# Longer lags between the stages of two rank-and-store passes of a graph kernel, and another order of the stages within a turn

## The chip, the cores and the metric

The kernel runs on one core of one Trainium2 chip. The metric is the device time of one execution, in microseconds. Three executions of the kernel before took 5831.21, 5831.95 and 5836.04 us; the median is 5831.95 us. Below, PE is the tensor engine, DVE the vector engine, ACT the scalar engine, POOL GpSimd, and SP the engine that issues most of the plain DMAs.

## What is computed

Four graph layers follow one another on 3125 nodes with 128 features and 53125 edges (25000 random edges, the same reversed, and a loop for each node, sorted by `dst`). Each layer is followed by a residual sum and a layer norm:

```python
edge_index = jnp.stack([src, dst])
x = _layernorm(x + _L0_gnn_ref(x, edge_index, edge_attr_32, ...), axis=-1)   # attention over dst, 8 heads
x = _layernorm(x + _L1_gnn_ref(x, src, dst, ...), axis=-1)                   # normalised sum over src
x = _layernorm(x + _L2_gnn_ref(x, edge_attr_64, edge_index, ...), axis=-1)   # attention over nodes and edges
x = _layernorm(x + _L3_gnn_ref(x, node_vec, ..., src, dst), axis=-1)         # two softmaxes over dst
```

The sums and maxima over segments need the edges grouped by `src` in some layers and by `dst` in others. The kernel therefore sorts the edges twice, ahead of all layers, and only these two sorting passes are touched by the change.

## The kernel before

**Tiles.** Edges are taken 128 to a tile and four tiles to a group (G = 4). The first pass ("src") has 104 groups, the second ("dst") has 110. A pass takes each group of 512 edge rows, works out the slot of each row among the rows with the same key (its rank), and scatters the rows into a table in HBM with one indirect DMA per tile.

**The stages of one group** are functions in `ranks` (L561 to L641) and are the same in both passes:

- `dve_onehots` (L571): DVE writes the one-hot matrices of the low key part, `so16` (L574), and of the high part, `hi16` (L576).
- `pe_transpose` (L603, matmuls of L609): PE turns `so16` over, into half of PSUM bank 2.
- `copy_out` (L631, L636): ACT copies that into `rohT_keys[k]`, of which there are four.
- `pe_same` (L612, L616): PE multiplies the turned one-hots with themselves, into bank 6 or 7.
- `dve_mask` (L580, L583): DVE masks the result into `ssame`.
- `pe_rank` (L620, L625 and L627): PE makes the slot numbers, into bank 3, of which there is one.
- `dve_pick` (L586, L589 and L595): DVE multiplies with `hi16` and reduces into `stage[k]`, four buffers. The reduction waits until the scatter of four groups earlier has landed.
- `scatter` (L651, L655) on POOL issues the four indirect DMAs of the group out of `pay[k]`, four buffers. `load` (L647) on SP fills `pay[k]` once the scatter of four groups earlier has landed.

In the first pass ACT has one more stage, `ids` (L671, L673). In the second pass `grown_rows` (L681 to L744) adds the key and value rows of the source node to each edge row:

- `onehots` (L692, L694) on DVE, `transposes` (L705, L709) on PE into the other half of bank 2, `copies` (L712, L715) on ACT.
- `kv` (L717, L723): PE first loads four block numbers into registers (L777), then does 12 matmuls of 257 columns into banks 0, 1, 4 and 5, one set for all groups, so it waits until `keep` of the group before is done.
- `keep` (L728, L732): two ACT copies out of those four banks into `pay[k]`, then, after a wait for `products`, one small copy (L737) that releases the scatter.
- `products` (L697, L699 and L702) on DVE.

**What sets the order.** Every engine executes its own list in order. `stepwise` (L537) gives each engine a list of pairs (lag, stage). In turn N the engine runs down its list, and a pair with lag d works on group N - d. Four turns are one body of a hardware loop (`run`, L348); two bodies are written out ahead of it (lead=2). Waits on semaphores tie the engines together. The two lists of the kernel before are

```python
return {"vector": [(4, dve_pick), (2, dve_mask), (0, dve_onehots)],                             # L639
        "tensor": [(1, pe_same), (3, pe_rank), (0, pe_transpose)], "scalar": [(0, copy_out)],
return loads, {"vector": [(3, products), (1, onehots)], "tensor": [(3, kv), (1, transposes)],   # L743
               "scalar": [(3, keep), (1, copies)]}, ready, (s_td, s_tc)
```

In the second pass `together` (L746) puts the list of `ranks` ahead of that of `grown_rows`. A turn is thus: PE `pe_same`, `pe_rank`, `pe_transpose`, `kv`, `transposes`; ACT `copy_out`, `keep`, `copies`; DVE `dve_pick`, `dve_mask`, `dve_onehots`, `products`, `onehots`.

**The shared bank.** PE must not write PSUM bank 2 while ACT reads it, and in the second pass two transposes land there. So `pe_transpose` of group n waits for `copies` of group n - 2 (L607: s_tc of the grown rows at n - 1), and `copy_out` of group n waits for `transposes` of group n - 1 (L634: s_td of the grown rows at n).

Of the kernel before, what the change touches and what calls it, by code (L numbers as in the profile page):

```python
# [25 lines left out]
P = 128  # L26
# [20 lines left out]
G = 4  # L47
# [8 lines left out]
def wait(eng, sem, value):  # L56

    if isinstance(value, int) and value <= 0:
        return
    eng.wait_ge(sem, value)  # L60
# [30 lines left out]
def gnn_program(nc, x, keys, edge_attr, node_vec, Wqkv, WeT, L1_kernel, L1_bias, W_node,  # L91
                W_nodeT, W_edge, W_edgeT, a_node, a_edge, L3_W, L3_b, out):
    ctx = ExitStack()
    with ctx:
# [466 lines left out]
        def ranks(o, bank_shared=None):  # L561
# [9 lines left out]
            def dve_onehots(v, n, k):  # L571
                wait(v, s_td, n - 1)
                wait(v, s_ps, n - 3)
                nc.vector.tensor_tensor(so16[k % 2][:, :, :], iota0[:, None, :].to_broadcast([P, G, P]),  # L574
                                        key[o]["lo"][:, bass.ds(n * G, G)].to_broadcast([P, G, P]), ALU.is_equal)
                nc.vector.tensor_tensor(hi16[k][:, :, :], iota0[:, None, 0:NH].to_broadcast([P, G, NH]),  # L576
                                        key[o]["hi"][:, bass.ds(n * G, G)].to_broadcast([P, G, NH]),
                                        ALU.is_equal).then_inc(s_oh, 1)

            def dve_mask(v, n, k):  # L580
                v.wait_ge(s_sd, n + 1)
                wait(v, s_gd, n - 1)
                nc.vector.tensor_tensor(ssame[k % 2][:, :, :], ps[6 + k % 2][:, :].rearrange("p (g n) -> p g n", g=G),  # L583
                                        after[:, None, :].to_broadcast([P, G, P]), ALU.mult).then_inc(s_su, 1)
# [18 lines left out]
            def pe_transpose(pe, n, k):  # L603
                pe.wait_ge(s_oh, n + 1)
                wait(pe, s_tc, n)
                if bank_shared:
                    wait(pe, bank_shared[1], n - 1)  # L607
                for j in range(G):
                    last = nc.tensor.transpose(turned(k)[:, j * P:(j + 1) * P], so16[k % 2][:, j, :], ident16[:, :])  # L609
                last.then_inc(s_td, 1)  # L610
# [20 lines left out]
            def copy_out(act, n, k):  # L631
                act.wait_ge(s_td, n + 1)
                if bank_shared:
                    wait(act, bank_shared[0], n)  # L634
                wait(act, s_gd, n - 3)
                nc.scalar.copy(rohT_keys[k][:, :, :], turned(k)[:, 0:G * P].rearrange("p (g n) -> p g n", g=G)) \  # L636
                  .then_inc(s_tc, 1)

            return {"vector": [(4, dve_pick), (2, dve_mask), (0, dve_onehots)],  # L639
                    "tensor": [(1, pe_same), (3, pe_rank), (0, pe_transpose)], "scalar": [(0, copy_out)],  # L640
                    "placed": s_ps}  # L641

        def scatter_rows(o, loads, to, width, ready, placed):
# [16 lines left out]

            return {"sync": [(0, load)], "pool": [(4, scatter)]}

        def own_rows():
# [14 lines left out]

            return loads, {"scalar": [(2, ids)]}, ready

        def grown_rows():  # L681

# [22 lines left out]
            def transposes(pe, n, k):  # L705
                pe.wait_ge(s_oh, n + 1)
                wait(pe, s_tc, n)
                for j in range(G):
                    last = nc.tensor.transpose(beside_ranks[:, j * P:(j + 1) * P], oh16[k % 2][:, j, :], ident16[:, :])  # L709
                last.then_inc(s_td, 1)  # L710
# [29 lines left out]
            def ready(g, n, k):  # L740
                hold(g, s_up, n + 1, passed["pool"])

            return loads, {"vector": [(3, products), (1, onehots)], "tensor": [(3, kv), (1, transposes)],  # L743
                           "scalar": [(3, keep), (1, copies)]}, ready, (s_td, s_tc)  # L744

# [610 lines left out]
        for c in range(5):  # L1356
            with nc.Block() as block:
                @block.vector
                def _(v):
# [5 lines left out]
        cleared = key_starts("dst", table2)  # L1365
        loads, parts, ready, turned_beside = grown_rows()
        placing = ranks("dst", turned_beside)
        run((stepwise("dst", together(placing, parts, scatter_rows("dst", loads, table2, ROW2, ready, placing["placed"])),
                      cleared), 0, T // (4 * G), 1), lead=2)
# [371 lines left out]
```

## Time and profile before

| what | before |
|---|---|
| median of three executions | 5831.95 us |
| the profiled execution's own time | 5880.84 us |
| its span from first to last instruction | 5879.0 us |
| PE busy / DVE busy / POOL busy / ACT busy | 51% / 41% / 38% / 15% of the span |
| first pass, first to last scatter | 236.5 to 880.8 us |
| second pass, first to last scatter | 1085.6 to 1811.5 us |
| granted PE clock over the whole span | 0.531 of full |

The profiled execution took 48.89 us more than the median. Every duration in this document that is not a run's time comes from such an execution. An engine can be idle because it waits for nothing that matters; the busy shares say only that no engine is full over the whole span, and the two passes have to be read by themselves.

### The profile page before, as it was taken

How to read it: one execution, taken by the hardware profiler on the slowest of the kernel's cores; microseconds unless marked ns; L12 is line 12 of the kernel's file. 1: busy time of each engine (PE TensorE's matmuls, PEld its weight loads, DVE VectorE, ACT ScalarE, POOL GpSimd, SP SyncE). 2: the span in 40 equal slices, each digit the busy share in tenths (PEclk: the TensorE clock that was granted, in tenths of full speed). 3: DMA queues.
4: the chain of work that ended last, by engine and by line, in shares of the span. 5: the costliest groups of instructions: out<-in, count | busy, mean ns of one | idle time of the engine just before them, and what ended most of it. 6: DMA issues, size and time to landing. Idle time of an engine off the chain costs nothing. (4 is left out here: it accounts for less than half of the span.)

```text
span 5879.0 us, 79222 instructions
## 1 busy us (share of the span) xinstructions
PE 3027.2 (51%) x17772; PEld 2505.0 (43%) x17773; DVE 2436.1 (41%) x5186; ACT 893.0 (15%) x2414; POOL 2253.2 (38%) x2513
## 2 busy tenths in 40 slices
PE   2222222466664555399756665333334999633332
PEld 1111111344443444289745555222223999423332
DVE  7733337655554444644522222422225555422224
ACT  1211111333332222100000000111111222100000
POOL 0266660466662000000047776366660000056763
PEclk6555555566665555555555555555555555555555
DMA  0122223444442222123211112122222334111112
GB/s 20 47 64 65 64 62 8 153 140 141 140 143 74 65 65 65 33 66 77 54 38 43 44 44 39 31 42 43 43 42 39 82 84 86 30 41 45 45 45 36
DMA packets 639690, 365.32 MB, mean 62 GB/s; under 512 B 456808, under 2 KB 589970, under 8 KB 639634
## 3 DMA queue, kind: packets, MB, share of 16 engines
q0 software_dynamic: 83712, 175.08, 10.9%
q1 hardware_dynamic: 381682, 131.90, 10.1%
q10 hardware_dynamic: 174240, 57.69, 4.2%
q8 instruction: 23, 0.38, 0.0%
q14 instruction: 33, 0.27, 0.0%
HBM read 229.22 MB, written 135.24 MB: 62 GB/s over the span
## 5 line engine op out<-in xcount | busy, mean ns | idle before, releaser
L1102 PE MATMUL banks<-both,pool 128*128 128x128 f32 x3520 | 1198.2, 478 | 423.1 <-DVE both L1681 423.1
L1102 PEld LDWEIGHTS banks<-both,pool 128*128 128x128 f32 x3520 | 918.5, 332 | 479.5 <-issue 455.5
L1066 POOL COPY stage<-slots 128x4 int32 (+1 forms) x220 | 43.0, 196 | 1921.4 <-ACTq L383 1920.2
L655 POOL DMA_INDIRECT table<-pay_own,stage x432 | 442.0, 1023 | 748.6 <-DVE stage L595 294.2
L1099 PEld LDWEIGHTS banks<-pool 128*128 128x128 f32 x1760 | 475.7, 330 | 288.9 <-issue 288.9
L1099 PE MATMUL banks<-pool 128*128 128x11 f32 (+1 forms) x1760 | 398.2, 299 | 255.6 <-DVE pool L1468 251.2
L761 POOL DMA_INDIRECT pool<-y_table,stage x440 | 445.2, 1012 | 188.9 <-issue 170.3
L761 POOL DMA_INDIRECT pool<-n_table,stage x440 | 438.3, 996 | 190.7 <-issue 154.3
L655 POOL DMA_INDIRECT table<-q,stage x424 | 431.5, 1018 | 188.6 <-issue 125.4
L761 POOL DMA_INDIRECT pool<-z_table,stage x440 | 430.6, 979 | 188.8 <-issue 116.8
L1078 DVE TENSOR_TENSOR pool<-iota,slots 128x512 f32<-128x512 f32 x440 | 302.7, 688 | 340.0 <-PE banks L1102 294.5
L616 PE MATMUL banks<-acc 128*128 128x128 bf16 x856 | 118.8, 286 | 596.2 <-ACT acc L636 310.0
L589 DVE TENSOR_TENSOR acc<-banks,acc 128x208 f32<-128x208 f32 x214 | 80.1, 374 | 742.6 <-PE banks L627 389.0
L616 PEld LDWEIGHTS banks<-acc 128*128 128x128 bf16 x856 | 67.5, 123 | 650.2 <-issue 442.8
L723 PE MATMUL banks<-pool,both 128*128 x1320 | 292.6, 407 | 30.2 <-issue 17.9
L1681 DVE TENSOR_TENSOR both<-pool,slot_tmp 128x512 f32<-128x512 f32 x110 | 76.2, 692 | 505.9 <-DMA pool<-z_table,stage 505.9
L636 ACT COPY acc<-banks 128x512 bf16<-128x512 bf16 x214 | 125.4, 586 | 1045.4 <-issue 430.4
L1025 ACT COPY acc<-banks 128x512 f32<-128x512 f32 (+1 forms) x12 | 5.0, 487 | 1767.2 <-PEq L383 1767.2
L1467 DVE TENSOR_SCALAR both<-pool 128x512 f32<-128x512 f32 x110 | 55.2, 502 | 524.3 <-DMA pool<-y_table,stage 524.3
L1102 PE MATMUL banks<-acc 128*128 128x64 f32 x880 | 242.1, 438 | 0.0
L1102 PEld LDWEIGHTS banks<-acc 128*128 128x128 f32 x880 | 235.6, 335 | 3.4
L723 PEld LDWEIGHTS banks<-pool,both 128*128 128x128 bf16 x1320 | 177.8, 135 | 119.0 <-issue 54.5
(333 smaller groups left out, 5668.3 us busy)
## 6 DMA issues: line engine op xcount, KB each, us to landing
pay_own<-table SPq DMA_DIRECT2D x110, 332.0 KB, 3.1
pool<-table ACTq DMA_DIRECT2D x110, 256.0 KB, 2.9
h_rows<-pool SPq DMA_DIRECT2D x110, 128.0 KB
acc<-table SPq DMA_DIRECT2D x110, 128.0 KB, 2.3
pool<-h_rows ACTq DMA_DIRECT2D x110, 128.0 KB, 2.9
pay_own<-table ACTq DMA_DIRECT2D x110, 128.0 KB, 2.6
pay_own<-table SPq DMA_DIRECT2D x56, 200.0 KB
q<-table SPq DMA_DIRECT2D x54, 200.0 KB
```

What stands on the lines that cost most here:

```text
L589: nc.vector.tensor_tensor(sprod[:, :, :].rearrange("p g (n s) -> p g n s", s=2), rank_bank(k).rearrange("p (g n s) -> p g n s", g=G, s=2), ...
L616: last = nc.tensor.matmul(ps[6 + k % 2][:, j * P:(j + 1) * P], rohT_keys[k][:, j, :], rohT_keys[k][:, j, :], start=True, stop=True)
L636: nc.scalar.copy(rohT_keys[k][:, :, :], turned(k)[:, 0:G * P].rearrange("p (g n) -> p g n", g=G)) \
L655: nc.gpsimd.indirect_dma_start(to, bass.IndirectOffsetOnAxis(ap=stage[k][:, j:j + 1], axis=0), pay[k][:, j, 0:width], None).then_inc(lande ...
L723: last = nc.tensor.matmul(kv_of[j], rohT[k % 2][:, j, :], kv16[:, bass.ds(blocks[j], 1), part, :].rearrange("p o d -> p (o d)"), start=par ...
L761: nc.gpsimd.indirect_dma_start(to, None, table_ap, bass.IndirectOffsetOnAxis(ap=index, axis=0)) \
L1066: nc.gpsimd.tensor_copy(stage[h][:, :], index[:, bass.ds(i * (2 * G) + h * G, G)]).then_inc(s_st, 1)
L1078: nc.vector.tensor_tensor(buf["oh"][h][:, :, :], iota1[:, None, :].to_broadcast([P, G, P]), lo1[o][:, t].to_broadcast([P, G, P]), ALU.is_e ...
L1099: nc.tensor.matmul(banks[:, bass.ds(blocks[j] * SIDE + (7 * 512 + side0), side_cols)], buf["oh"][h][:, j, :], buf["side"][h][:, j, 0:side_ ...
L1102: last = nc.tensor.matmul(banks[:, bass.ds(blocks[j] * P + col0, cols)], buf["oh"][h][:, j, :], buf["rhs"][h][:, j, 0:cols], start=False, ...
L1467: nc.vector.tensor_scalar(rhs[h][:, :, :], grow[h][:, :, 0:D], 1.0, None, ALU.mult)
L1681: return nc.vector.tensor_tensor(rhs[h][:, :, :], grow[h][:, :, 0:D], bc(slot_tmp[0][:, t], [P, G, D]), ALU.mult)
```

## The change

Seven things are edited. (1) In `ranks` the lags become 6, 4, 0 on DVE, 3, 5, 1 on PE and 2 on ACT. (2) The one-hot `hi16` moves from `dve_onehots` to `dve_mask`, with its wait for `stage` of four groups earlier. (3) `pe_transpose` waits for the grown `copies` one group further back, and `copy_out` for the grown `transposes` one group further back. (4) The grown `transposes` get a new wait, for `copy_out` of group n + 1 (s_tc of the ranks at n + 2). (5) The grown lags become 5 and 2 on DVE, 5 and 3 on PE, 6 and 4 on ACT. (6) The lags of `ids` and `scatter` become 5 and 7. (7) In the second pass a hand-written `order` replaces the plain joining of lists: PE now runs `pe_same`, `pe_rank`, `kv`, `pe_transpose`, `transposes`; ACT `keep`, `copy_out`, `copies`; DVE `dve_pick`, `dve_mask`, `products`, `onehots`, `dve_onehots`.

```diff
             def dve_onehots(v, n, k):
                 wait(v, s_td, n - 1)
+                nc.vector.tensor_tensor(so16[k % 2][:, :, :], iota0[:, None, :].to_broadcast([P, G, P]),
+                                        key[o]["lo"][:, bass.ds(n * G, G)].to_broadcast([P, G, P]),
+                                        ALU.is_equal).then_inc(s_oh, 1)
+
+            def dve_mask(v, n, k):
                 wait(v, s_ps, n - 3)
-                nc.vector.tensor_tensor(so16[k % 2][:, :, :], iota0[:, None, :].to_broadcast([P, G, P]),
-                                        key[o]["lo"][:, bass.ds(n * G, G)].to_broadcast([P, G, P]), ALU.is_equal)
+                wait(v, s_gd, n - 1)
                 nc.vector.tensor_tensor(hi16[k][:, :, :], iota0[:, None, 0:NH].to_broadcast([P, G, NH]),
-                                        key[o]["hi"][:, bass.ds(n * G, G)].to_broadcast([P, G, NH]),
-                                        ALU.is_equal).then_inc(s_oh, 1)
-
-            def dve_mask(v, n, k):
+                                        key[o]["hi"][:, bass.ds(n * G, G)].to_broadcast([P, G, NH]), ALU.is_equal)
                 v.wait_ge(s_sd, n + 1)
-                wait(v, s_gd, n - 1)
                 nc.vector.tensor_tensor(ssame[k % 2][:, :, :], ps[6 + k % 2][:, :].rearrange("p (g n) -> p g n", g=G),
...
                 if bank_shared:
-                    wait(pe, bank_shared[1], n - 1)
+                    wait(pe, bank_shared[1], n - 2)
...
                 if bank_shared:
-                    wait(act, bank_shared[0], n)
+                    wait(act, bank_shared[0], n - 1)
...
-            return {"vector": [(4, dve_pick), (2, dve_mask), (0, dve_onehots)],
-                    "tensor": [(1, pe_same), (3, pe_rank), (0, pe_transpose)], "scalar": [(0, copy_out)],
+            return {"vector": [(6, dve_pick), (4, dve_mask), (0, dve_onehots)],
+                    "tensor": [(3, pe_same), (5, pe_rank), (1, pe_transpose)], "scalar": [(2, copy_out)],
+                    "copied": s_tc,
...
-            return {"sync": [(0, load)], "pool": [(4, scatter)]}
+            return {"sync": [(0, load)], "pool": [(7, scatter)]}
...
-            return loads, {"scalar": [(2, ids)]}, ready
+            return loads, {"scalar": [(5, ids)]}, ready
...
                 pe.wait_ge(s_oh, n + 1)
                 wait(pe, s_tc, n)
+                pe.wait_ge(ranks_copied[0], min(n + 2, groups_of["dst"]) if isinstance(n, int) else n + 2)
...
-            return loads, {"vector": [(3, products), (1, onehots)], "tensor": [(3, kv), (1, transposes)],
-                           "scalar": [(3, keep), (1, copies)]}, ready, (s_td, s_tc)
+            return loads, {"vector": [(5, products), (2, onehots)], "tensor": [(5, kv), (3, transposes)],
+                           "scalar": [(6, keep), (4, copies)]}, ready, (s_td, s_tc)
...
-        run((stepwise("dst", together(placing, parts, scatter_rows("dst", loads, table2, ROW2, ready, placing["placed"])),
+        ranks_copied.append(placing["copied"])
+        order = {"vector": [placing["vector"][0], placing["vector"][1], parts["vector"][0], parts["vector"][1], placing["vector"][2]],
+                 "tensor": [placing["tensor"][0], placing["tensor"][1], parts["tensor"][0], placing["tensor"][2], parts["tensor"][1]],
+                 "scalar": [parts["scalar"][0], placing["scalar"][0], parts["scalar"][1]]}
+        run((stepwise("dst", together(order, scatter_rows("dst", loads, table2, ROW2, ready, placing["placed"])),
```

No buffer is added: every tile and every instruction of a group stays, and only their order and their waits differ.

## Rows read from the trace of the kernel before

**Rows 1.** Busy time by stretch; columns: stretch, length, PE, PEld, DVE, ACT, POOL, clock, DMA, GB/s

```profile
237.00:882.00 645.00, 149.10 (x1616) 116.98 (x1616) 211.79 (x505) 70.80 (x202) 412.68 (x416) 0.50 0.23 64
1085.00:1813.00 728.00, 481.51 (x3448) 339.49 (x3448) 371.57 (x857) 231.98 (x541) 460.36 (x440) 0.64 0.44 141
```

**Rows 2.** Instructions of L655, both passes: duration in ns min/median/max, first and last start

```profile
L655 POOL DMA_INDIRECT table<-pay_own,stage x208: 956/962/1479, 236.5 to 870.7; - x104
L655 POOL DMA_INDIRECT table<-q,stage x208: 955/962/1422, 247.5 to 880.8; - x104
...
L655 POOL DMA_INDIRECT table<-pay_own,stage x224: 955/963/1336, 1085.6 to 1811.5; - x112
```

**Rows 3.** Groups by line, 442 to 842 us: busy, mean ns | idle before, releasers

```profile
L655 POOL DMA_INDIRECT table<-pay_own,stage x129 | 129.3, 1002 | 105.9 <-DVE stage L595 75.7 <-issue 30.2
```

**Rows 4.** POOL's timeline, first pass: start, us, engine, line; idle time before

```profile
657.12 0.96 POOL L655 DMA_INDIRECT table<-q,stage  x1 [0.30 <-issue]
663.02 1.10 POOL L655 DMA_INDIRECT table<-pay_own,stage  x1 [4.94 <-DVE stage L595]
```

**Rows 5.** DVE's timeline, first pass, the two picks before that gap

```profile
650.80 0.38 DVE L589 TENSOR_TENSOR acc<-banks,acc 128x208 f32<-128x208 f32 x1 [7.29 <-remote]
...
661.04 0.38 DVE L589 TENSOR_TENSOR acc<-banks,acc 128x208 f32<-128x208 f32 x1 [8.07 <-PE banks L627]
```

**Rows 6.** PE's timeline, same stretch

```profile
643.63 0.58 PE L609 MATMUL banks<-ident,acc 128*128 128x128 bf16 x4
659.25 0.61 PE L616 MATMUL banks<-acc 128*128 128x128 bf16 x4 [15.04 <-issue]
```

**Rows 7.** ACT's timeline, same stretch

```profile
658.61 0.59 ACT L636 COPY acc<-banks 128x512 bf16<-128x512 bf16 x1 [15.79 <-remote]
```

**Rows 8.** Groups by line, 1200 to 1700 us

```profile
L655 POOL DMA_INDIRECT table<-q,stage x152 | 159.7, 1051 | 81.2 <-issue 41.6 <-ACT ge_src L737 39.5
```

**Rows 9.** PE's timeline, second pass, one turn and the start of the next

```profile
1642.78 0.61 PE L616 MATMUL banks<-acc 128*128 128x128 bf16 x4 [3.26 <-ACT acc L636]
...
1643.51 0.22 PE L627 MATMUL banks<-acc 128*128 128x26 bf16 x1
1644.27 0.61 PE L609 MATMUL banks<-ident,acc 128*128 128x128 bf16 x4 [0.53 <-ACT both L715]
1644.97 2.76 PE L723 MATMUL banks<-pool,both 128*128 x12
1647.52 0.52 PE L709 MATMUL banks<-ident,both 128*128 128x128 bf16 x4
1648.84 0.40 PE L616 MATMUL banks<-acc 128*128 128x128 bf16 x4 [0.81 <-issue]
...
1651.25 1.04 PE L723 MATMUL banks<-pool,both 128*128 x4 [0.37 <-issue]
```

**Rows 10.** ACT's timeline, second pass, same stretch

```profile
1642.06 0.59 ACT L636 COPY acc<-banks 128x512 bf16<-128x512 bf16 x1 [6.13 <-issue]
...
1648.20 0.59 ACT L636 COPY acc<-banks 128x512 bf16<-128x512 bf16 x1 [3.99 <-PE banks L709]
1648.69 1.09 ACT L732 COPY pay_own<-banks 128x514 f32<-128x514 f32 x2
```

**Rows 11.** POOL's timeline, second pass

```profile
1651.94 1.25 POOL L655 DMA_INDIRECT table<-pay_own,stage  x1 [0.30 <-issue]
...
1656.99 0.96 POOL L655 DMA_INDIRECT table<-q,stage  x1 [0.97 <-issue]
```

**Rows 12.** DVE's timeline, second pass, beside those scatters

```profile
1651.68 0.68 DVE L574 TENSOR_TENSOR acc<-iota,raw 128x512 bf16<-128x512 f32 x1
...
1652.45 0.42 DVE L699 TENSOR_TENSOR acc<-q,wge 128x256 f32<-128x256 f32 x1
...
1653.24 0.68 DVE L694 TENSOR_TENSOR both<-iota,slots 128x512 bf16<-128x512 f32 x1
```

**Rows 13.** Instructions of L574, second pass: first and last start

```profile
L574 DVE TENSOR_TENSOR acc<-iota,raw x110: 679/682/733, 1071.8 to 1777.0; 128x512 bf16<-128x512 f32 x110
```

More of the change, by code:

```diff
@@ L572, in dve_onehots @@
                 wait(v, s_td, n - 1)
-                wait(v, s_ps, n - 3)
                 nc.vector.tensor_tensor(so16[k % 2][:, :, :], iota0[:, None, :].to_broadcast([P, G, P]),
-                                        key[o]["lo"][:, bass.ds(n * G, G)].to_broadcast([P, G, P]), ALU.is_equal)
-                nc.vector.tensor_tensor(hi16[k][:, :, :], iota0[:, None, 0:NH].to_broadcast([P, G, NH]),
-                                        key[o]["hi"][:, bass.ds(n * G, G)].to_broadcast([P, G, NH]),
+                                        key[o]["lo"][:, bass.ds(n * G, G)].to_broadcast([P, G, P]),
                                         ALU.is_equal).then_inc(s_oh, 1)
             def dve_mask(v, n, k):
+                wait(v, s_ps, n - 3)
+                wait(v, s_gd, n - 1)
+                nc.vector.tensor_tensor(hi16[k][:, :, :], iota0[:, None, 0:NH].to_broadcast([P, G, NH]),
+                                        key[o]["hi"][:, bass.ds(n * G, G)].to_broadcast([P, G, NH]), ALU.is_equal)
                 v.wait_ge(s_sd, n + 1)
-                wait(v, s_gd, n - 1)
                 nc.vector.tensor_tensor(ssame[k % 2][:, :, :], ps[6 + k % 2][:, :].rearrange("p (g n) -> p g n", g=G),
@@ L677, in ready, with grown_rows @@
                 hold(g, s_id, n + 1, passed["pool"])
-            return loads, {"scalar": [(2, ids)]}, ready
-        def grown_rows():
+            return loads, {"scalar": [(5, ids)]}, ready
+        def grown_rows(ranks_copied):
             s_pl = [sem(f"sorted_rows_loaded{k}") for k in range(4)]
@@ L1365, in gnn_program @@
         cleared = key_starts("dst", table2)
-        loads, parts, ready, turned_beside = grown_rows()
+        ranks_copied = []
+        loads, parts, ready, turned_beside = grown_rows(ranks_copied)
         placing = ranks("dst", turned_beside)
-        run((stepwise("dst", together(placing, parts, scatter_rows("dst", loads, table2, ROW2, ready, placing["placed"])),
+        ranks_copied.append(placing["copied"])
[3 more added lines that the diff above has]
+        run((stepwise("dst", together(order, scatter_rows("dst", loads, table2, ROW2, ready, placing["placed"])),
                       cleared), 0, T // (4 * G), 1), lead=2)
```

## The prediction

> **What bounds it now.** The busy shares name no bound, so the two touched passes are read by stretch: POOL is busy for 413 of 645 us in the first and 460 of 728 in the second, and PE, at half its clock in the first and 0.64 in the second, for 149 and 482 [rows 1]. POOL's work is the scatters. First to last start is 644.3 us in the first pass, over 103.75 groups (the last start is the fourth of a group) 6.21 us a group, and 725.9 us in the second, over 109.75 groups 6.61 [rows 2]. Against this stand POOL's own times. A scatter takes 1.002 us on average in the steady part of the first pass [rows 3] and 1.051 in the second [rows 8], with 0.30 between two of them [rows 4, 11]. Four make 5.21 and 5.40 us a group: the floor that POOL sets. What lies above it, 1.00 and 1.21 us a group, is waiting: 104 and 133 us. Nothing else in the kernel is touched.
>
> **First pass: who is late?** In one loop body of four groups (25 us) POOL runs back to back and then idles 4.94 us for the slot numbers in `stage` [rows 4]. Its supplier, DVE's pick, waited 7.29 us and then 8.07 us for `pe_rank` [rows 5]. PE's rows show the transposes of a group issued at 643.63, but ACT, which waits only for them, starts at 658.61, after 15.79 us idle; PE's next row is at 659.25 [rows 6, 7]. So PE's results came 14.4 us after the modelled end of its work, though no engine owed it anything. What holds PE there no row says. I call it the gap; a pass of 26 bodies has about one each.
>
> **Second pass: who is late?** Here PE and ACT take turns. The row of `kv` is 2.76 us; then PE waits 0.81 for ACT's `copy_out`, and its `pe_transpose` waits 0.53 for ACT's `copies` [rows 9]. ACT in turn starts `copy_out` only when PE's `transposes`, behind `kv`, are done (releaser L709, 3.99 idle), and `keep` (1.09 us) stands behind it [rows 10]. The bank that the two transposes share makes each engine finish its turn before the other starts: 6.06 us from 1642.78 to 1648.84. POOL idles 0.97 before the next group [rows 11].
>
> **The change, part by part.** The sum is made against the profiled execution (5880.84 us); it lies 48.89 above the median of 5831.95, and I carry the difference over unchanged.
>
> (a) *Second pass, lags, order and the two relaxed waits.* With the transposes of one turn released by the copies of the same turn, but `kv` put ahead of them, ACT's `keep`, `copy_out` and `copies` run beside PE's `pe_same`, `pe_rank` and `kv`. `kv` needs only `keep` of the group before, which starts when the previous `kv` ends and takes 1.09; PE has two sets of transposes and two small stages, 2.08 us by [rows 9] (0.95, 0.61, 0.52), in between. The new wait of `transposes` for `copy_out` is met too: ACT is through with its turn two copies of 0.59 [rows 7, 10] after PE's last turn, while PE is in `kv`. Behind it on PE stand `pe_same` and `pe_rank`, which DVE's pick needs a turn later, so a turn of slack covers them. PE then waits for nobody and is bound by its work: from 1642.78 to 1643.73, and from 1644.27 to 1648.04, 4.72 us [rows 9]. To this comes the load of the block numbers, until now under the transposes but for 0.37 us [rows 9]; behind `pe_rank` it is bare, between 0.37 and 0.75 us (that row and its cover of 0.38), and I take 0.5: 5.2. The gap exists here also, smaller: `copy_out` found 6.13 instead of 3.99 us idle, 2.14 more [rows 10], about once in four groups, 0.5 a group. Together 5.7, a little above POOL's 5.40. I take 5.7: (6.61 - 5.7) x 110 = -100 us. Ends: 5.40, POOL's floor, if the gap hides in the four buffers or PE's clock is granted more often: -133. And 6.3, where only the 0.53 and no more of the waits goes: -34.
>
> (b) *First pass, lags.* Work and buffers stay; one bank still holds the ranks, so PE can't run ahead of the pick. `pe_rank` no longer stands behind a `pe_same` whose copy has just been made. After the gap ACT's copy (0.59) and the start of `pe_same` came first: copy at 658.61, `pe_same` at 659.25 [rows 6, 7]. That start, 0.64 us, goes once in a body: 26 x 0.65 = -17 us. Ends: 0, and -104 if the gap itself came from the order and POOL reaches its floor.
>
> (c) *`hi16` moved to the mask stage.* The same instruction on DVE, which is busy 51% of the second pass [rows 1]; its wait for `stage` is met two turns earlier. Nothing, and 0.26 us of DVE a group has that idle half as cover.
>
> (d) *`scatter` and `ids` lags 7 and 5.* Per-engine bookkeeping; POOL's list has one stage, and SP's loads keep lag 0, their place and their wait, so each queue issues as before. Nothing in the steady state.
>
> (e) *Filling.* The first scatter came 13.8 us after the first one-hots, with lag 4 [rows 2, 13]: 3.45 a turn. Two more turns are at most 7 us a pass, 14 in all; the first turns do less work, so I take 10. At the end POOL drains last either way. Ends: 0 and 14.
>
> Sum: -100 - 17 + 10 = -107; 5880.84 becomes 5774, the median 5725.
>
> **A rule against it.** Scatters beside DVE work are longer, 1.25 us against 0.96, but the neighbours of that row run through three DVE instructions at no more than this [rows 11, 12]. By the rows the cost is fixed per group and is in the 5.40. The Trainium skill (SBUF — State Buffer, Who interferes with whom) says that a DVE instruction with two SBUF inputs and a GpSimd instruction that reads SBUF take an exclusive port, the loser blocked for the whole instruction. That rule would matter more the closer the two engines are packed; by it the sum would be that of rival 5.
>
> **Rivals.**
> 1. *The gap belongs to the old order.* PE sat at a wait for ACT while it lasted [rows 6]; if it needs that, both passes reach POOL's floor: -104 - 100 or -133, + 10, 5605 to 5638. For it: the busier PE of the second pass has a short gap, not a long one. Against it: the waits in other turns of the first pass cost nothing.
> 2. *PE and ACT still alternate.* If sharing the bank binds through the new wait, a turn is 6.3: -34 - 17 + 10, 5791. Against it: the waits name stages a turn back.
> 3. *Slower: the long gap moves into the second pass.* There PE is to be the bound, and nothing hides a gap. The place is `kv` behind `pe_rank`. Four turns are 4 x 5.2 + g; the old four are 26.4, so it decides from g = 5.6 us. With the 8.07 of [rows 5] four turns are 28.9, 7.22 a group: +67 - 17 + 10, 5892. Against it: today's second pass has 2.14.
> 4. *The change does nothing*, as another wait binds PE and ACT at the old pace: 5832, within 6.
> 5. *Slower, the port.* DVE's three instructions of [rows 12], 0.68 + 0.42 + 0.68, each blocking POOL in full on top of 4 x (0.96 + 0.30) = 5.04, make 6.82 a group: +23, with (b) and (e) 5848. Today's scatters bear out a fifth of it.
>
> **How the numbers follow.** Forecast 0.55; rivals 1 to 5: 0.20, 0.15, 0.05, 0.03, 0.02. A measurement of this kernel tells 0.2%, some 12 us, from no change. Faster: 0.90; same: 0.03; slower: 0.07. The forecast's own ends of (a) and (b) give about 5690 to 5765. The range takes in rival 2, and rival 1 down to 5620, where its better half starts; outside stay that half and the slow cases, under 0.2: 5620 to 5805.
>
> **What would show it.** In the second pass: PE's `pe_transpose` no longer released by L715, `kv` rows directly behind L627, a turn of 5.2 to 5.7 us, ACT starting `keep` ahead of `copy_out`, scatters 5.4 to 5.8 us a group. In the first pass: the 15 us without a PE row still there, POOL's idle time about 4.3 instead of 4.94, 6.0 to 6.1 a group. I am wrong if the first pass loses its gap, if PE's turns stay above 6 us, or if the time between the passes moves.

## The result and the profile after

Over five executions of each, the kernel before took 5836.04 us (median; 5831.21 to 5842.58) and the changed one 5862.96 us (5859.70 to 5868.44): ratio 1.0046, 95% interval 1.0031 to 1.0061. The change made the kernel **0.46% slower**, where 1.8% faster was predicted and 5620 to 5805 us was the range.

The profiled execution of after took 5864.28 us (span 5862.5). That of before took 5880.84, some 45 more than its median, so the two profiles side by side show a gain of 16.6 us where the medians show a loss of 27. The stretches have to be compared with this in mind.

The two passes of after by stretch and its scatters, first pass, then second; they answer to [rows 1, 2]:

```profile
237.00:925.00 688.00, 181.67 (x1740) 128.26 (x1740) 240.32 (x578) 79.89 (x234) 410.97 (x416) 0.50 0.29 61
1085.00:1800.00 715.00, 386.58 (x3334) 301.46 (x3331) 365.27 (x832) 224.05 (x521) 429.68 (x424) 0.74 0.44 139
```

```profile
L656 POOL DMA_INDIRECT table<-pay_own,stage x208: 955/962/1429, 236.2 to 852.8; - x104
L656 POOL DMA_INDIRECT table<-q,stage x208: 955/962/1470, 247.3 to 862.9; - x104
```

```profile
L656 POOL DMA_INDIRECT table<-pay_own,stage x224: 957/963/1452, 1066.1 to 1806.6; - x112
...
  ACT ge_src L739: 371.1, 53
  issue: 123.1, 385
```

The first pass takes 862.9 - 236.2 = 626.7 us (before 644.3), the second 1806.6 - 1066.1 = 740.5 (before 725.9). In the second, POOL waits 53 times for ACT's small copy (L739), once in two groups; the 371.1 us contain some 203 between the passes (1066.1 - 862.9), so a wait is (371.1 - 203.2) / 52 = 3.2 us. Counted in the two traces, POOL stops for more than 2 us between two scatters 18 times in the second pass of before and 52 times in that of after. POOL's timeline shows the pattern, eight scatters back to back and then a stop (answers to [rows 11]):

```profile
1432.88 0.96 POOL L656 DMA_INDIRECT table<-q,stage  x1 [3.23 <-ACT ge_src L739]
...
1440.95 0.96 POOL L656 DMA_INDIRECT table<-q,stage  x1 [0.31 <-issue]
1442.21 0.96 POOL L656 DMA_INDIRECT table<-q,stage  x1 [0.30 <-issue]
```

The PE, ACT and DVE timelines of the same turns (answer to [rows 9, 10, 12]):

```profile
1436.43 2.03 PE L725 MATMUL banks<-pool,both 128*128 x12
1438.30 0.38 PE L609 MATMUL banks<-ident,acc 128*128 128x128 bf16 x4
1438.52 0.39 PE L711 MATMUL banks<-ident,both 128*128 128x128 bf16 x4
...
1440.44 0.20 PE L627 MATMUL banks<-acc 128*128 128x26 bf16 x1
1445.78 0.61 PE L725 MATMUL banks<-pool,both 128*128 x2 [5.14 <-ACT pay_own L734]
```

```profile
1435.01 1.08 ACT L734 COPY q<-banks 128x514 f32<-128x514 f32 x2 [1.97 <-PE banks L725]
...
1444.45 1.08 ACT L734 COPY pay_own<-banks 128x514 f32<-128x514 f32 x2 [7.29 <-remote]
```

```profile
1444.61 0.69 DVE L695 TENSOR_TENSOR both<-iota,slots 128x512 bf16<-128x512 f32 x1 [2.68 <-remote]
```

The turn is the one that was planned: `kv` (L725), both transposes, and `keep` first on ACT. But `kv` ends at 1438.46 by the model and `keep`, which waits for it and for the load of its rows, starts at 1444.45; that load was issued at 1426.44, 18 us before, and in no group of this pass less than 15 us before; the transposes issued at 1438.52 (L711) release DVE only at 1444.61. PE had issued all of it by 1440.44. By the signals in the trace the results of `kv`, both transposes, `pe_same` and `pe_rank` came at 1444.38, 1444.43, 1444.49, 1444.55 and 1444.65, 1.2 to 1.5 us after POOL's last scatter ended (1442.21 + 0.96 = 1443.17). The rows of those transposes are 0.22 us apart, the signals 0.06: the work had been done, and its results were held. It is not this turn alone: of the 110 `keep` stages of this pass, 55 start more than 2 us after both `kv`'s modelled end and ACT's own last instruction, and 48 of these 55 start 1.2 to 1.5 us after the end of POOL's last scatter; only two start while POOL goes on issuing. This is the gap of the prediction, 6 us long, once in **two** groups: the cycle from 1432.88 to the next start after a stop, 1446.44, is 13.56 us, 6.78 a group. The Trainium skill (Perfetto Trace Analysis, Tensor Engine Instruction) says that a matmul's end in a profile is estimated, and that its semaphore is pushed only when PSUM has acknowledged the write. The trace agrees in so far as the modelled end came 6 us ahead of the first reader.

### The profile page after: what moved, and what is told of

Same layout as the page of the kernel before. It is cut to its first block and busy times, and to the rows that moved or that the text cites. A ratio compares the mean times of both kernels' runs of the same rounds, so it can differ in the third digit from the quotient of the medians.

```text
span 5862.5 us, 79114 instructions
## 1 busy us (share of the span) xinstructions
PE 2965.0 (51%) x17772; PEld 2482.8 (42%) x17773; DVE 2436.9 (42%) x5186; ACT 896.3 (15%) x2414; POOL 2239.7 (38%) x2513
## 5 line engine op out<-in xcount | busy, mean ns | idle before, releaser
L725 PE MATMUL banks<-pool,both 128*128 x1320 | 252.6, 362 | 239.1 <-ACT pay_own L734 127.8
L625 PE MATMUL banks<-work,acc 128*128 (+1 forms) x856 | 123.3, 219 | 367.3 <-issue 183.5
L725 PEld LDWEIGHTS banks<-pool,both 128*128 128x128 bf16 x1320 | 160.9, 122 | 301.9 <-issue 247.7
L625 PEld LDWEIGHTS banks<-work,acc 128*128 128x128 bf16 x856 | 86.3, 108 | 406.3 <-issue 399.2
L609 PE MATMUL banks<-ident,acc 128*128 128x128 bf16 x856 | 117.0, 283 | 239.7 <-ACT acc L636 120.5
```

Of the source, the lines that this page charges most:

```text
L625: nc.tensor.matmul(to, rohT_keys[k][:, j, :], pairs[o][:, :, bass.ds(n * G + j, 1), :] .rearrange("p h t s -> p h (t s)"), start=True, sto ...
L725: last = nc.tensor.matmul(kv_of[j], rohT[k % 2][:, j, :], kv16[:, bass.ds(blocks[j], 1), part, :].rearrange("p o d -> p (o d)"), start=par ...
```

## The experiments

The kernel before itself has two times, on one and the same chip and unchanged: about 5670 us when PE's results come in time, and 5830 to 5872 when they come late during the scatters. Kernels that were timed together on one chip, within some minutes, make one occasion here. Each run below stands beside the kernel before of its own occasion; "first" and "second" are the times from first to last scatter start of the passes, out of its profile. "Late" and "in time" are told from the traces: where the kernel before takes 5670 us, no copy of the transposes in the first pass (L636) starts more than 0.2 us after both the modelled end of the transposes and ACT's own last instruction; where it takes 5830 or more, 36 to 52 of the 104 start more than 2 us after them, in every run but e13.

| occasion | kernel | median us | ratio (95%) | first | second |
|---|---|---|---|---|---|
| record, late | before | 5836.0 | | 644.3 | 725.9 |
| | full change | 5863.0 | 1.0046 (1.0031–1.0061) | 626.7 | 740.5 |
| 1, in time | before (e1: 5671.4, one execution) | 5669.7 | | 539.2 | 666.0 |
| | e2 first pass only | 5672.3 | 1.0001 (0.9991–1.0012) | 542.3 | 665.2 |
| | e3 second pass only | 5584.4 | 0.9849 (0.9836–0.9863) | 540.0 | 579.5 |
| | e4 narrow rows | cut off | | 543.5 | 588.4 |
| 2, in time | e5 full change | 5583.2 | 0.9847 (0.9833–0.9861) | 543.3 | 581.7 |
| | e6 lags only | 5661.1 | 0.9985 (0.9976–0.9994) | 542.9 | 651.7 |
| 3, late (before 5871.7) | e7 full, more PE work | 6049.9 | 1.0302 (1.0282–1.0322) | 637.5 | 913.9 |
| | e8 before, more PE work | 5982.1 | 1.0187 (1.0168–1.0207) | 643.1 | 835.2 |
| | e9 order only | 5929.4 | 1.0096 (1.0077–1.0116) | 642.3 | 788.0 |
| 4, late (before 5833.3) | e10 full change | 5859.8 | 1.0047 (1.0030–1.0064) | 624.7 | 739.5 |
| | e11 lags only | 5834.7 | 1.0001 (0.9990–1.0011) | 624.9 | 717.4 |
| | e12 narrow rows | cut off | | 625.4 | 737.6 |
| | e13 all landed | 6024.6 (one run) | | 712.0 | 818.4 |
| 5, in time (before 5668.7) | e14 three landed | 5703.8 | 1.0062 (1.0045–1.0079) | 582.7 | 658.3 |
| | e15 small instruction | 5719.1 | 1.0088 (1.0071–1.0104) | 610.7 | 646.3 |
| 6, in time (before 5668.0) | e16 three landed | 5702.1 | 1.0061 (1.0044–1.0078) | 582.1 | 657.4 |
| | e17 order only | 5618.1 | 0.9909 (0.9892–0.9925) | 539.4 | 614.6 |
| 7, late (before 5830.8) | e18 three landed | 5793.9 | 0.9930 (0.9914–0.9947) | 620.7 | 687.6 |

Occasions 2, 3, 6 and 7 were on the same chip, within an hour: in time, late, in time, late, the last two less than three minutes apart.

### One pass at a time (e1 to e4)

e1 is the kernel before. e2 and e3 choose the old or the new lags, waits, order and place of `hi16` by pass:

```diff
+NEW = {"src": True, "dst": False}      # e2; e3 the other way round
...
-                    wait(pe, bank_shared[1], n - 2)
+                    wait(pe, bank_shared[1], n - (2 if NEW[o] else 1))
```

> The kernel before, unchanged, for a second profile. The first profiled execution took 5880.84 us against a median of 5836. Theory A (the second pass slowed by more than the first gained, and the first profile of before was a slow example): this execution takes about 5836 us, its passes are some 10 to 45 us shorter than in the first profile (first pass under 644, or second under 726 us from first to last scatter). Theory B (the passes are as in the first profile, and the change loses time elsewhere): the passes again take 644 and 726 us, whatever the total.

> Only the first pass has the new lags; the second is as before. Theory A: the first pass gains a little (first to last scatter about 627 us as in the profile of the changed kernel), so the time is 10 to 20 us below before. Rival B (the deeper lags cost in both passes): 5 to 20 us above before.

> Only the second pass has the new lags, order and waits; the first is as before. Theory A: the second pass holds the loss, 35 to 50 us above before (27 measured for both plus what the first pass gained). Rival B: about half of the 27 us, 10 to 15 above before.

None of the three expected pictures came, because the gap was gone and with it 166 us of the kernel before. The first pass takes 539.2 / 103.75 = 5.20 us a group there, POOL's floor as predicted (5.21), with nothing left to gain. The second gains 86.5 us and lands at 579.5 / 109.75 = 5.28, its floor. So the change does what it was meant to do, and the loss on record is not in its turns as such.

e4 cuts the changed kernel off behind the second pass (all four layers are left out) and lets the second pass write 16 columns of each row to a narrow table:

```diff
-                    nc.gpsimd.indirect_dma_start(to, ...
-                                                 pay[k][:, j, 0:width], None)
+                    nc.gpsimd.indirect_dma_start(thin if o == "dst" else to, ...
+                                                 pay[k][:, j, 0:16 if o == "dst" else width], None)
```

> The changed kernel, ended after the second pass (all four layers left out), whose scatters put only 16 of 358 columns of each row into a narrower table: as many scatter instructions on POOL, a twentieth of their bytes. Theory T (PE's results are held back by the traffic of the scatters): in the second pass the gap of about 6 us between the issue of kv and ACT's keep in every second group goes, and a group takes 5.0 to 5.6 us. Theory P (they are held back by POOL's own scatter instructions, or by the order of the waits): the gap stays, two groups still take about 13.5 us.

Where nothing is late it says nothing about the gap; e12 is the same kernel on a late occasion.

### The whole change, and its lags without its order (e5, e6)

```diff
+        order = together(placing, parts)      # e6
         run((stepwise("dst", together(order,
```

> The whole change, unchanged, in the same comparison as the next kernel. Theory A: the change is worth what its second pass is worth (5584.4 against 5669.7 us, -85), since on the chip of the last runs the first pass already runs at POOL's pace: ratio 0.985, no stretch without PE rows, second pass 5.3 us a group. Theory B: the two longer passes disturb each other or the place where the second starts: ratio above 0.99 though PE's results come in time. Theory C: this is a chip where PE's results come late during the scatters, as in the two traces on record: kernel before near 5836 us, ratio 1.003 to 1.006, and results of PE come late once in two groups in the second pass.

> The whole change but for its hand-written order: in the second pass the lists are joined plainly, so PE runs pe_transpose ahead of kv, ACT copy_out ahead of keep. Theory L, the longer lags alone take PE and ACT out of each other's turns: as the full change, second pass 5.3 us a group (ratio 0.985 where PE's results come in time). Theory O, kv has to stand ahead of the transposes, or PE waits with it for keep of the same turn and ACT for PE: second pass 6.0 us a group or more, ratio 1.00 or a little below.

e5 is theory A: 0.9847. Its scatters and their waits in the second pass; POOL's idle time is nearly all its own 0.30 us between scatters:

```profile
L656 POOL DMA_INDIRECT table<-pay_own,stage x224: 957/963/1488, 983.3 to 1565.0; - x112
...
  ACT ge_src L739: 203.6, 6
  issue: 125.0, 410
```

Nearly all of the 203.6 us in 6 waits is the time between the passes (983.3 - 780.2 = 203.1). PE, ACT and POOL in one turn of e5:

```profile
1419.82 0.63 PE L609 MATMUL banks<-ident,acc 128*128 128x128 bf16 x4
1420.25 0.63 PE L711 MATMUL banks<-ident,both 128*128 128x128 bf16 x4
...
1422.45 1.68 PE L725 MATMUL banks<-pool,both 128*128 x12 [0.49 <-ACT both L717]
```

```profile
1420.12 1.08 ACT L734 COPY pay_own<-banks 128x514 f32<-128x514 f32 x2 [4.24 <-PE banks L725]
...
1424.22 1.08 ACT L734 COPY pay_own<-banks 128x514 f32<-128x514 f32 x2 [1.96 <-PE banks L725]
```

```profile
1419.40 0.96 POOL L656 DMA_INDIRECT table<-q,stage  x1 [0.30 <-issue]
...
1424.47 0.96 POOL L656 DMA_INDIRECT table<-q,stage  x1 [0.31 <-issue]
```

`keep` starts 0.10 us after `kv`'s modelled end (1418.74 + 1.28 = 1420.02), where in after it starts 6 us late. e6 comes out near theory O (6.0 us a group or more): without the order PE and ACT take turns again, 5.94 us a group. PE and ACT of e6:

```profile
1431.62 0.38 PE L609 MATMUL banks<-ident,acc 128*128 128x128 bf16 x4 [1.75 <-ACT both L717]
...
1434.92 0.63 PE L711 MATMUL banks<-ident,both 128*128 128x128 bf16 x4
```

```profile
1435.64 0.58 ACT L636 COPY acc<-banks 128x512 bf16<-128x512 bf16 x1 [4.17 <-issue]
```

This is rival 2 of the prediction, for the lags alone: `pe_transpose` ahead of `kv` waits for the copies, and ACT idles 4.17 us behind `kv` before `copy_out`.

### More work for PE, and the order alone (e7, e8, e9)

```diff
-                for j in range(G):                                          # pe_same
+                for j in list(range(G)) * (13 if o == "dst" and k % 2 else 1):
```

> The whole change, and in the second pass pe_same of every second group repeats its four matmuls 13 times in place of once (same result), some 5 us more of PE at half its clock, which is what the trace of the changed kernel on record shows PE's results late by, once in two groups. Theory G, that lateness alone accounts for its 740.5 us: the pass goes from 580 us to between 700 and 760 (two groups 13 to 13.8 us), the kernel to about 5700 to 5770. Theory S, the buffers and longer lags swallow a stall of this size: the pass stays below 620 us.

> The kernel before with the same repeated matmuls. If PE and ACT alternate there, nothing hides them: the pass grows by all of it, 55 times some 5 us: from 666 to about 900 us or more, ratio 1.04. Then the lateness on record, which costs the old order only 60 us in this pass and the new order 160, is no fixed stall of PE: it depends on how closely the scatters follow one another. Rival: the old order hides it as well and lands near 726 us, as on record; then the lateness is a fixed stall.

> The kernel before with the hand-written order of the second pass alone: kv ahead of pe_transpose, keep ahead of copy_out, lags, waits and hi16 as before. Theory O, the order does it: near the full change, second pass 580 to 600 us, ratio 0.985 to 0.99. Theory B, order and lags only work together: pe_transpose still waits for the copies of the turn before and copy_out for the transposes of its own turn, so a turn stays at 5.9 to 6.1 us, second pass 650 to 670 us, ratio 0.997 to 1.001.

This was a late occasion (before 5871.7). e7 and e8 were meant to imitate the gap where there is none; with a real gap beside it they settle little. Both sizes missed: 913.9 instead of 700 to 760, and 835.2 instead of 900. What they do show is that added PE work is not hidden by either order: beside the record's passes 173 us more in the new one and 109 in the old, over 55 pairs of groups 3.2 and 2.0 us. Part of the added work was paid back by the clock: PE's granted clock in the pass was 0.79 and 0.78, against 0.74 in after and 0.64 in before.

e9 tells more. The order with the old lags costs 62 us here (788.0 against the record's 725.9; by the medians of this occasion 58). It had been expected to change nothing or to gain. POOL stops for more than 2 us 68 times in the second pass, 18 times in before. 73 of the 110 `keep` stages start more than 1 us after `kv`'s modelled end and ACT's own last instruction, most of them 0.7 to 1.1 us after POOL's last scatter ended: the late result is there again, shorter, and in two groups of three.

### The record repeated, and what holds PE's results (e10 to e13)

> The whole change once more. If this is an occasion on which PE's results come late (kernel before near 5870 us, first pass 643 us), theory A expects the result on record: a second pass of about 740 us, kernel 5860 to 5900, ratio 0.998 to 1.006. If the kernel before takes 5670 us: 5583, ratio 0.985. A ratio of 0.985 beside 5870 would say that the lateness does not decide.

> The whole change without its hand-written order (as e6). Where PE's results come late, the order alone cost 62 us in the second pass (788.0 against 725.9). Theory O, the order is what loses: lags alone give 700 to 726 us in the second pass and the gain of 17 in the first, kernel 20 to 40 us faster than before, ratio 0.993 to 0.997. Theory L, the longer lags lose too, because more groups are ready and POOL runs longer unbroken: 735 us or more, ratio 1.00 or above.

> The changed kernel cut off behind the second pass; there the scatters write 16 columns of each row into a narrow table (all layers left out, so only the passes are compared). Theory T, the traffic of the scatters holds PE's results: none late in the second pass, and it falls to POOL's floor, 580 to 595 us, while the first pass, with full rows, still has them late and takes 627 us. Theory P, POOL's unbroken instructions hold them, whatever they move: second pass 700 us or more with two groups in 13 us, as on record.

e10 is the record again: 1.0047, passes of 624.7 and 739.5, one stop of POOL in two groups:

```profile
1427.12 0.96 POOL L656 DMA_INDIRECT table<-pay_own,stage  x1 [0.30 <-DVE stage L595]
1431.39 0.96 POOL L656 DMA_INDIRECT table<-q,stage  x1 [3.31 <-ACT ge_src L739]
...
1440.72 0.96 POOL L656 DMA_INDIRECT table<-q,stage  x1 [0.30 <-issue]
1444.93 0.96 POOL L656 DMA_INDIRECT table<-pay_own,stage  x1 [3.25 <-ACT ge_src L739]
```

e11: with the lags alone the second pass takes 717.4, 22 us less than with the order; the sum is 1.0001, above the 0.993 to 0.997 that theory O expected. Beside e6 this shows the order's two faces: 70 us gained where results come in time (651.7 to 581.7), 22 lost where they come late.

e12 falsifies theory T. With rows of 16 columns the second pass is as slow, and stops as with full rows (53 stops of more than 2 us, against 51 in e10):

```profile
L657 POOL DMA_INDIRECT thin<-pay_own,stage x224: 952/958/1440, 1064.2 to 1801.8; - x112
...
  ACT ge_src L740: 370.3, 55
```

```profile
1417.66 0.96 POOL L657 DMA_INDIRECT thin<-pay_own,stage  x1 [3.38 <-ACT ge_src L740]
...
1426.84 0.96 POOL L657 DMA_INDIRECT thin<-pay_own,stage  x1 [0.30 <-issue]
1431.21 1.24 POOL L657 DMA_INDIRECT thin<-q,stage  x1 [3.42 <-ACT ge_src L740]
```

e13 adds a pause to POOL:

```diff
                 ready(g, n, k)
+                wait_scattered(g, o, n - 1, (k - 1) % 4, passed["pool"])
```

> The whole change, and POOL waits before the scatters of each group until those of the group before have landed. Theory P: with such a pause in each group no result of PE is late by more than one group's scatters (5 us), and those that are come at the pause; POOL's stretches of 16 or 20 scatters in the first pass are gone, and it takes 104 times 6.3 to 7 us, 655 to 730. Rival: lateness of 10 us and more stays, so it does not end because POOL stops.

On the same late occasion POOL now runs in steps of four scatters with an idle time of 2.1 us in the first pass and 2.4 in the second, and the stops for the suppliers are gone:

```profile
1421.67 0.96 POOL L657 DMA_INDIRECT table<-pay_own,stage  x1 [2.50 <-DMA table<-q,stage]
...
1429.13 0.95 POOL L657 DMA_INDIRECT table<-pay_own,stage  x1 [2.40 <-DMA table<-pay_own,stage]
...
1436.59 0.97 POOL L657 DMA_INDIRECT table<-q,stage  x1 [2.41 <-DMA table<-pay_own,stage]
```

Late results are all but gone. In the first pass 42 of 104 `copy_out` stages of e10 start more than 2 us after the transposes' modelled end and ACT's own last instruction (up to 19.0 us), none in e13 (0.5 us at most). In the second 55 of 110 `keep` stages do in e10 (up to 7.2 us), 5 in e13 (3.6 at most; there `keep` starts some 2.6 us after the load of its rows is issued, and so may be waiting for that). This is counted from the rows, since many records of PE's signals are missing from e13's trace. It rests on one execution. First pass 712.0 / 103.75 = 6.86 us a group, as theory P expected.

### How short a pause will do (e14 to e18)

```diff
+                wait_scattered(g, o, n - 1, (k - 1) % 4, passed["pool"], G - 1)      # e14, e16, e18
```

```diff
+                nc.gpsimd.memset(spare[:, :], 0.0).then_inc(s_sp, 1)                 # e15
+                hold(g, s_sp, n + 1, passed["pool"])
```

> The whole change, and POOL waits before each group until three of the four scatters of the group before have landed. All four cost an idle time of 2.1 us; a scatter is issued every 1.27 us, so three should cost 0.8. Theory P with short pauses being enough: few late results, first pass 104 x (4 x 0.96 + 3 x 0.30 + 0.8), 576 to 600 us, second pass 630 to 660; on an occasion with late results (kernel before 5830 to 5870) 100 to 120 us faster than before, ratio 0.978 to 0.983, and about 1.00 where the kernel before takes 5670. Rival, a pause must be longer than 1 us to help: late results stay, first pass 625 us or more, second 730 or more, ratio 1.00 or above.

> The whole change, and ahead of each group's scatters POOL writes one column of an unused tile and waits for its own write. If the end of the indirect DMAs' issue is what lets PE's results through, some 0.3 to 0.6 us a group does it, and both passes come near POOL's floor plus that: 570 to 600 and 620 to 650 us, ratio 0.976 to 0.983 where results come late. If POOL has to be idle, or for longer than this: passes as with the full change, 625 and 740 us or more, ratio 1.00 to 1.01.

> As e14. On an occasion with late results (kernel before 5830 to 5870): if a pause of 0.8 us is enough, the kernel takes the same 5704 us as without lateness, passes 583 and 658, ratio 0.972 to 0.978; if it is not, passes of 625 or more and 730 or more, ratio 1.00 or above. Where the kernel before takes 5670: 1.006 again.

> As e9, the hand-written order with the old lags. Where results come late: second pass 788 again, ratio 1.010. Where they come in time (kernel before 5670): if order and lags only work together, a turn of 5.9 to 6.1 us, second pass 650 to 670, ratio 0.997 to 1.001; if the old lags under the new order make PE and ACT wait for each other more (keep, copy_out, copies, then pe_same, all in one turn), 680 to 760, ratio 1.003 to 1.016, and the loss seen in e9 is that of the order and not of the lateness.

> As e14 and e16, for an occasion with late results (kernel before 5830 to 5870): 5704 us and ratio 0.972 to 0.978 if the pause of 0.8 us is enough; first pass 625 us or more, second 730 or more and a ratio of 1.00 or above if it is not. Where the kernel before takes 5670, 1.006 once more, and the question stays open.

Occasions 5 and 6 were in time, so e14 to e16 show the price of the pause only: in e14 and e16 some 0.82 us of idle time in place of 0.30, and 582.7 and 658.3 us for the passes, a kernel 0.6% slower than before; in e15 1.01 us and a kernel 0.9% slower. e17 missed both of its cases (650 to 760 us). It completes the square for the second pass in time: before 666.0, lags alone 651.7, order alone 614.6, both 581.7. The order alone gains 51 us there, so its loss in e9 belongs to the late occasion and not to the order as such.

e18 caught a late occasion: 5793.9 against 5830.8, ratio 0.993. That is between the two cases I had named. POOL and ACT in the second pass of e18:

```profile
1431.15 0.96 POOL L657 DMA_INDIRECT table<-q,stage  x1 [0.99 <-DMA table<-q,stage]
...
1437.03 0.96 POOL L657 DMA_INDIRECT table<-pay_own,stage  x1 [0.80 <-issue]
...
1440.82 0.96 POOL L657 DMA_INDIRECT table<-pay_own,stage  x1 [0.30 <-issue]
1445.17 0.96 POOL L657 DMA_INDIRECT table<-pay_own,stage  x1 [3.39 <-issue]
```

```profile
1442.81 1.08 ACT L735 COPY pay_own<-banks 128x514 f32<-128x514 f32 x2 [7.67 <-remote]
```

PE's result again comes about 1 us after POOL's last scatter (1440.82 + 0.96 = 1441.78, `keep` at 1442.81). But POOL had then gone through seven groups, since 1401.39, without a stop over 1.2 us; in e10 it stops after two. Over the second pass it stops for more than 2 us 9 times, against 51 in e10. Late results are still many: 52 `copy_out` in the first pass (42 in e10) and 42 `keep` in the second (55 in e10), up to 14.3 and 8.4 us. 19 of those 42 `keep` start while POOL goes on issuing, so a result does not always wait for POOL to stop; the same is seen in the first pass of before, for 19 of its 42 late copies. A pause of 0.8 us helps, and 2.1 us removes nearly all lateness but costs more than it gives. Where results come late e18 beats the kernel before by 0.7%, while the full change, measured on other late occasions, loses 0.5% to it; where they come in time the same pause loses to both (5702 us in e16, against 5668 for before and 5583 in e5). No version tried beats both on both kinds of occasion.

## Why the prediction was wrong

**(a) The failed step is the gap's term in the second pass**: "The gap exists here also, smaller: [...] about once in four groups, 0.5 a group". I took a wait of unknown cause from the old order and carried it over as a fixed amount. Without the gap the relaxed waits do what the step said: 6.07 us a group becomes 5.28 to 5.30, a gain of 84 to 87 us, and what binds is POOL's floor, not PE. Two sizes were off, to the same side: the floor, put at 5.40 from scatters of 1.051 us, is 5.26 with the 1.015 of e3, and PE's bare work, put at 5.2, did not bind: a turn ran in 4.1 us in places (`keep` 1420.12 to 1424.22 in e5), and the granted clock was 0.81 of full (0.64 in e1). With the gap it becomes 740.5 / 109.75 = 6.75, because the gap did not keep its size. PE's results are held while POOL issues scatters back to back, and the one that POOL's next group hangs on is read 0.5 to 1.5 us after POOL has stopped: 0.5 in [rows 4, 7] (658.08 to 658.61), 1.3 in after, 1.0 in e18, though its modelled end lay 14.4, 6.0 and 8.4 us back. A fixed delay would not keep to POOL's stops like that. The old order made POOL pause about 1 us after each group of four [rows 11]. That these pauses let the results through at a small price fits e13 and e18, where added pauses do so, but it was not tried on the old order itself. The new one keeps POOL supplied: eight scatters in a row, so the result is held until POOL has run dry, POOL waits 3.2 us for what follows from it, and the cycle repeats.

**The rival that happened is rival 3**, to which I gave 0.05: the gap grew in the second pass, where PE had no slack. Its place was right (`kv`, whose result `keep` waits for). Its size was not: it foresaw 7.22 us a group with one gap of 8.07 in four groups; measured are two of about 6, and 6.75, and four new groups take 2 x 13.56 = 27.1 us against the old 26.4. "Against it: today's second pass has 2.14" was the same mistake as in (a).

**Rival 1** has its other half: the two passes do reach POOL's floor once the gap is gone, but occasions take it away, not the order. **Rival 5**, the port: in time, with POOL packed at its floor, a scatter takes 1.015 (e3) and 1.020 us (e5) on average in the second pass, against 1.008 in e1. DVE did the same work in both, and full blocking by its three instructions would have added 0.45 us to each scatter, so that is excluded as a price of the closer packing. Rival 2 is what the lags do alone (e6). Rival 4 did not occur.

**(b)** -17 was predicted for the first pass and -17.6 measured between the two profiled executions (e10: 624.7 us), but that is luck: not for the reason given. POOL's timeline of after, first pass (answers to [rows 4]):

```profile
601.99 1.29 POOL L656 DMA_INDIRECT table<-pay_own,stage  x1 [3.24 <-DVE stage L595]
...
632.26 1.29 POOL L656 DMA_INDIRECT table<-pay_own,stage  x1 [4.62 <-ACT q L674]
...
663.01 1.33 POOL L656 DMA_INDIRECT table<-q,stage  x1 [5.04 <-DVE stage L595]
```

The idle time is 4.6 to 5.0 us as before, not 4.3. What changed is how far POOL runs between two of them: mostly 20 scatters, 16 before, so that the pass has 21 stops of some 4.2 us in place of 26. In time there is nothing to gain, and e2 measures 0 (1.0001).

**(c), (d)**: not tried by themselves; e3 and e5 leave no room for a cost of either. **(e)** was 10 us too dear: from the last scatter of the first pass to the first of the second are 203.2 us after and 204.8 before, and the first scatter of all comes at 236.2 and 236.5. More turns of filling cost nothing that can be seen.

**The sum.** The profiled executions give -17.6 + 14.6 for the passes and -13.6 elsewhere; the last lies in one later stretch that the change does not touch, the gather from `n_table` (696.6 us before, 682.3 after; 654.9 in e1, so it too is longer where results come late). The medians give +27. By subtraction, and so an estimate: outside the passes the late executions of after, e10 and e11 spend 4495.3, 4493.6 and 4502.7 us. An execution of before of 5836.0 us (span some 5834.2) would then have 1331 to 1341 us in its passes, where after has 626.7 + 740.5 = 1367.2: a loss of 27 to 36 us in the two together, about what the medians say. How it divides between them isn't shown, since there is no profile of such an execution of before: the record's took 5880.84 us, and e8 and e9, whose first passes also take 642 to 643 us, come from an occasion on which before took 5871.7. So the 17.6 us of the first pass isn't sure for an ordinary late execution either, and the loss in the second is larger than the 14.6 us by whatever of the surplus of the record's profile lay there.

**What stays open**: what the late occasions are. They came and went on the same chip within minutes, with unchanged code. That the lateness hangs on how closely POOL's scatters follow one another is shown by e13, and e12 excludes the width of what they move; which path between PE and its readers is held isn't shown. Nor is it shown what lets some results through while POOL goes on issuing. It is also open whether another instruction on POOL would do as well as idling, since e15 met no late occasion.

## What to carry to other kernels

A wait without an owner must not go into a sum as a constant: find out first what it ends with (here: the late result that mattered came about 1 us after the neighbour engine's last scatter), and cost the change by what it does to that. When a fix removes an engine's small pauses, ask who was served in them. And profile the kernel before on more than one occasion: it had two times 3% apart, and the same change gains 1.5% beside the one and loses 0.5% beside the other.

## What the runs showed of the hardware

- On one chip the kernel before took 5669.9, 5871.7, 5668.0 and 5830.8 us (medians) on four occasions. Of the 209 us between the profiled executions of e1 and the record, 207 lie in stretches in which POOL issues indirect DMAs: 105 us in the first pass, 60 in the second and 42 in one later stretch of L761 (696.6 against 654.9 us).
- While POOL issues indirect DMAs back to back, PE's results can reach ACT and DVE 6 us late in the second pass and 14 in the first [rows 6, 7], several at once, on some occasions and not on others; with 2.1 us of idle time after every four scatters almost none is late (e13), with 0.8 us many still are, but POOL stops for them less often (e18). The width of the scattered rows (16 columns or all) makes no difference: 737.6 and 739.5 us.
- PE's granted clock in the second pass was 0.64 of full in the old order, 0.74 in the new one with late results, and 0.81 with results in time, with less PE busy time for the same matmuls (460 us in e1, 386 in e5, over stretches with about as many matmuls, 3332 and 3308).
